# Softmax denominators of the first attention layer: from eight rows and a spreading product to all rows, inverted on GpSimd

## What is computed

```python
q = (layernorm(x) @ Wq)                 # 16 heads x 56 rows = 896 columns per batch
k, v = ctx @ Wk, ctx @ Wv               # 8 key/value heads
scores = einsum('bhtd,bhsd->bhts', q, k) / sqrt(128)
attn = softmax(scores, axis=-1)         # over 1500 context rows
out = einsum('bhts,bhsd->bhtd', attn, v) @ Wo
```

## Time and profile before

| what | us |
|---|---|
| median of 3 runs | 2184.47 (2183.3 to 2184.73) |
| the profiled execution, its own time | 2184.68 |
| its span, first to last instruction | 2182.9 |
| TensorE busy | 2129.5 (98%) |
| VectorE busy | 1566.5 (72%) |
| GpSimd busy | 1350.9 (62%) |
| ScalarE busy | 951.6 (44%) |

### The profile page before, as it was taken

One profiled execution on the slowest core, in us unless ns is written; L12 is line 12 of the kernel. 1 busy time (PEld: TensorE's weight loads), 2 busy tenths in 40 slices (PEclk: granted clock), 3 DMA queues, 4 the chain that ended last, 5 costly groups with the idle time before them and its releaser, 6 DMA issues. The chain is left out here.

```text
span 2182.9 us, 27103 instructions
## 1 busy us (share of the span) xinstructions
PE 2129.5 (98%) x8898; PEld 1565.0 (72%) x8898; DVE 1566.5 (72%) x2574; ACT 951.6 (44%) x2536; POOL 1350.9 (62%) x1056
## 2 busy tenths in 40 slices
PE   7999999999999999999999999899999999999999
PEld 6777777777777777777777655566666666665998
DVE  4689888988898888988896433656666666652577
ACT  3454454444444455444445225444444343431432
POOL 0378777877687767877787300088778787771221
PEclk9999999999999999999999999999999999999999
DMA  3000000000000000000001410011110111101110
GB/s 131 15 29 15 29 29 15 15 29 29 15 15 29 29 15 25 19 29 15 29 11 39 145 40 0 21 50 49 37 57 29 57 44 42 43 1 51 37 52 25
DMA packets 15134, 75.62 MB, mean 35 GB/s; under 512 B 1746, under 2 KB 2114, under 8 KB 13986
## 3 DMA queue, kind: packets, MB, share of 16 engines
q1 hardware_dynamic: 14994, 73.89, 10.4%
HBM read 72.97 MB, written 0.92 MB: 34 GB/s over the span
## 5 line engine op out<-in xcount | busy, mean ns | idle before, releaser
L618 POOL TENSOR_TENSOR l_prod<-l_prod 125x256 f32<-125x256 f32 x576 | 417.2, 738 | 270.6 <-DVE l_prod L683 270.0
L683 DVE TENSOR_TENSOR l_prod<-l_side,xq 125x512 f32<-125x512 f32 x576 | 394.5, 685 | 55.7 <-PE l_side L814 48.8
L959 POOL TENSOR_TENSOR l_acc<-l_acc,l_probs 125x896 f32<-125x896 f32 x160 | 346.0, 2163 | 81.4 <-ACT l_probs L909 65.6
L559 ACT ACTIVATE l_probs<-l_slots,mask_bias 125x448 f32<-125x448 f32 x384 | 238.1, 632 | 343.0 <-PE l_slots L753 342.9
L979 DVE TENSOR_TENSOR l_scaled<-l_slots,rk 125x896 f32<-125x896 f32 x192 | 207.0, 1084 | 197.8 <-PE l_slots L1044 197.6
L612 POOL TENSOR_TENSOR l_acc<-l_acc,l_probs 125x896 f32<-125x896 f32 x160 | 338.5, 2116 | 0.0
L541 ACT ACTIVATE l_prod_act<-l_prod_act 125x128 f32<-125x128 f32 x768 | 228.0, 298 | 235.5 <-DVE l_prod_act L683 235.4
L909 ACT ACTIVATE l_probs<-l_scaled 125x896 f32<-125x896 f32 x192 | 182.8, 952 | 320.7 <-DVE l_scaled L979 295.7
L692 DVE TENSOR_REDUCE l_msq<-l_prod 125x4 f32<-125x256 f32 x576 | 234.6, 410 | 1.6
L646 DVE SCALAR_TENSOR_TENSOR top<-l_side,mask_bias,top 125x448 f32<-125x448 f32 x330 | 223.1, 676 | 6.7 <-PE l_side L797 5.8
L1042 PE MATMUL l_slots<-l_qhi,l_clo 128*125 128x448 f32 x384 | 203.0, 529 | 1.4 <-DVE l_qlo L984 1.4
(11 more groups left out here) (241 smaller groups left out, 4374.6 us busy)
## 6 DMA issues: line engine op xcount, KB each, us to landing
land<-in_ctxT SPq DMA_DIRECT2D x32, 750.0 KB, 4.4
l_nat<-in_ctxN SPq DMA_DIRECT2D x16, 750.0 KB
post_we<-in_experts SPq DMA_DIRECT2D x20, 384.0 KB, 3.0
spare<-in_ctxN SPq DMA_DIRECT2D x8, 750.0 KB
nat<-in_ctxN SPq DMA_DIRECT2D x8, 750.0 KB
spare<-in_wo SPq DMA_DIRECT2D x2, 2048.0 KB, 7.8
spare<-in_wqT SPq DMA_DIRECT2D x4, 512.0 KB, 4.3
mid_fac<-in_factors SPq DMA_DIRECT2D x1, 2048.0 KB, 8.0
```

Of the source, the lines that this page charges most:

```text
L559: act.activation(P[t % NP][:, HALF * i:HALF * i + HALF], bank_of("S", t, i)[0:KT, 0:HALF], ACT.Exp, bias=m.mask_bias[:, b, t:t + 1]).then_ ...
L618: pool.tensor_tensor(buf[:, :, 0:C // 2], buf[:, :, 0:C // 2], buf[:, :, C // 2:C], ALU.add).then_inc(s.half_sum, 1)
L683: dve.tensor_tensor(to[:, :, :], bank, xt.unsqueeze(1).to_broadcast([KT, 4, C]), ALU.mult).then_inc(s.side_dve, 1)
L959: pool.tensor_tensor(acc[:, :], acc[:, :], P[t % NP][:, :], ALU.add).then_inc(s.acc, 1)
```

## The change

Bank "D" becomes two banks, one for each half. `sums` is now two products with an all-ones matrix (128 output rows, 448 columns each), so that the denominators stand on all rows at once, both at t = 0. `spread`, `m.inv` and VectorE's `invert` and `normalise` are gone. ScalarE copies both banks to a new SBUF buffer `den` at the start of step 1 (`sums_out`), ahead of the exponentials of tile 2. GpSimd then, in four pieces of 224 columns, one in each of the steps 6 to 9 between its `add` and its halvings, raises `den` to the power -1 and multiplies `qs` by it. For the last batch the four pieces follow behind the loop. In `ORDER` the entries "D", "E", "E" become "D", "D" and an unused one. `NPROD` goes from 5 to 4.

```diff
-NPROD, NPROD_ACT, LAG_N, NLOW = 5, 2, 3, 4
+NPROD, NPROD_ACT, LAG_N, NLOW = 4, 2, 3, 4
-ORDER = [("S", 0, 0), ("S", 0, 1), ("S", 1, 0), ("S", 1, 1), ("D", 0, 0), ("E", 0, 0), ("E", 0, 1)]
+ORDER = [("S", 0, 0), ("S", 0, 1), ("S", 1, 0), ("S", 1, 1), ("D", 0, 0), ("D", 0, 1), ("-", 0, 0)]
...
-                if kind == "D" and b > 0:
-                    return pe.wait_ge(s.inv, b)
-                if kind == "E" and b > 0:
-                    return pe.wait_ge(s.o_done, 2 * b - 1 + half)
+                if kind == "D" and b > 0:
+                    return pe.wait_ge(s.den_out, 2 * b - 1 + half)
...
+            def sums_out(b):
+                for half in range(2):
+                    act.wait_ge(s.den, 2 * b + half + 1)
+                    need(act, s.o_done, 4 * b)
+                    act.activation(den[:, half, :], bank_of("D", 0, half)[:, 0:HALF], ACT.Copy).then_inc(s.den_out, 1)
...
                 for t in range(NT):
+                    if t == 1 and b > 0:
+                        sums_out(b - 1)
...
+            sums_out(B - 1)
...
+            def normalise(b, i):
+                pool.wait_ge(s.o_raw, b + 1)
+                pool.wait_ge(s.den_out, 2 * b + i // 2 + 1)
+                cols = slice(HALF // 2 * i, HALF // 2 * (i + 1))
+                o = m.qs[:, b, :, :].rearrange("p h q -> p (h q)")[:, cols]
+                part = den[:, :, :].rearrange("p a c -> p (a c)")[:, cols]
+                pool.tensor_tensor(part, part, neg[:, :].to_broadcast([C, HALF // 2]), ALU.pow).then_inc(s.inv, 1)
+                pool.wait_ge(s.inv, 4 * b + i + 1)
+                pool.tensor_tensor(o, o, part, ALU.mult).then_inc(s.o_done, 1)
...
                     if t > 0:
                         add(b, t)
+                    if b > 0 and 6 <= t < 10:
+                        normalise(b - 1, t - 6)
...
+            for i in range(4):
+                normalise(B - 1, i)
...
-            def invert(b):
-                dve.wait_ge(s.den, b + 1)
-                dve.reciprocal(m.inv[0:QBLK, :], bank_of("D", 0, 0)[0:QBLK, 0:TT]).then_inc(s.inv, 1)
-            def normalise(b):
-                dve.wait_ge(s.o_raw, b + 1)
-                o = m.qs[:, b, :, :].rearrange("p (a h) q -> p a (h q)", a=2)
-                for half in range(2):
-                    dve.wait_ge(s.spread, 2 * b + half + 1)
-                    dve.tensor_tensor(o[:, half, :], bank_of("E", 0, half)[:, 0:HALF], o[:, half, :],
-                                      ALU.mult).then_inc(s.o_done, 1)
...
             def sums(b):
                 pe.wait_ge(s.acc, (NT - 1) * (b + 1))
-                wait_bank(pe, b + 1, "D", 0, 0)
-                for j in range(QBLK):
-                    last = pe.matmul(out[:, 0:TT], m.row_of[0:KT, 127 - j:255 - j], acc[:, TT * j:TT * j + TT],
-                                     start=j == 0, stop=j == QBLK - 1)
-            def spread(b):
-                ...
+                for half in range(2):
+                    wait_bank(pe, b + 1, "D", 0, half)
+                    pe.matmul(bank_of("D", 0, half)[:, 0:HALF], m.ones[0:KT, :], acc[:, HALF * half:HALF * half + HALF],
+                              start=True, stop=True).then_inc(s.den, 1)
```

More of the change, by code:

```diff
@@ L286, in side_job @@
                     if t == 0:
-                        dve.wait_ge(s.const, 5)
+                        dve.wait_ge(s.const, 4)
                         dve.tensor_scalar(m.top[:, cols], bank[0:KT, 0:HALF], bias, None, ALU.add).then_inc(s.side_dve, 1)
@@ L312, in _ @@
             dve.memset(m.ones_r[:, :].bitcast(F32), 1.0).then_inc(s.const, 1)
-            dve.memset(m.inv[:, :], 0.0).then_inc(s.const, 1)
             dve.memset(m.eps[:, :], RMS_EPS).then_inc(s.const, 1)
@@ L439, in first_attention @@
         "ld_land", "ld_nat0", "ld_nat1", "ctx_hi", "ctx_lo", "q_hi", "q_lo", "nat_hi", "xq", "shift",
-        "scores", "probs", "pv", "acc", "den", "inv", "spread", "o_raw", "o_done",
+        "scores", "probs", "pv", "acc", "den", "den_out", "neg", "inv", "o_raw", "o_done",
         "ld_wv", "ld_wo", "side_pe", "side_dve", "side_act", "half_sum", "sum_dve", "sum_act", "rk_pre"])
@@ L459, in first_attention @@
         msq = sb("msq", [KT, NT, H], F32)
+        den = sb("den", [C, 2, HALF], F32)
+        neg = sb("neg", [C, 1], F32)
         side = [psum(f"side{i}", [128, 512]) for i in range(3)]
@@ L606, in add @@
                 if t == 1:
-                    need(pool, s.den, b)
+                    need(pool, s.den, 2 * b)
                     pool.tensor_tensor(acc[:, :], P[0][:, :], P[1][:, :], ALU.add).then_inc(s.acc, 1)
@@ L618, in halve @@
                 pool.tensor_tensor(buf[:, :, 0:C // 2], buf[:, :, 0:C // 2], buf[:, :, C // 2:C], ALU.add).then_inc(s.half_sum, 1)
+            def normalise(b, i):
[7 more added lines that the diff above has]
+                pool.tensor_tensor(o, o, part, ALU.mult).then_inc(s.o_done, 1)
+            pool.memset(neg[:, :], -1.0).then_inc(s.neg, 1)
+            pool.wait_ge(s.neg, 1)
             for b in range(B):
@@ L726, in _ @@
                             jobs = jobs[1:]
-                        invert(b - 1)
                         twice_less_high(b)
-                    if t == 1 and b > 0:
-                        normalise(b - 1)
                     for n in jobs:
@@ L735, in _ @@
                             add_up(b, i)
-            invert(B - 1)
-            normalise(B - 1)
         @block.tensor
@@ L768, in sums @@
                 pe.wait_ge(s.acc, (NT - 1) * (b + 1))
-                wait_bank(pe, b + 1, "D", 0, 0)
-                out = bank_of("D", 0, 0)
-                for j in range(QBLK):
-                    last = pe.matmul(out[:, 0:TT], m.row_of[0:KT, 127 - j:255 - j], acc[:, TT * j:TT * j + TT],
-                                     start=j == 0, stop=j == QBLK - 1)
-                last.then_inc(s.den, 1)
-            def spread(b):
-                pe.wait_ge(s.inv, b + 1)
-                for half in range(2):
[L780 to L785, removed]
+                for half in range(2):
+                    wait_bank(pe, b + 1, "D", 0, half)
+                    pe.matmul(bank_of("D", 0, half)[:, 0:HALF], m.ones[0:KT, :], acc[:, HALF * half:HALF * half + HALF],
+                              start=True, stop=True).then_inc(s.den, 1)
             def side_job(n):
@@ L826, in side_jobs @@
                         del jobs[:count]
-                    if t == 1 and b > 0:
-                        spread(b - 1)
                     for half in range(2):
@@ L840, in _ @@
             sums(B - 1)
-            spread(B - 1)
 def second_attention(nc, m, a, tag, sem):
@@ L1761, in build @@
         m.row_of = sb("row_of", [128, 255], F32)
-        m.inv = sb("inv", [128, TT], F32)
         m.eps = sb("eps", [128, 1], F32)
```

## The result

The changed kernel takes 4408.29 us (median of 4 runs, 4405.93 to 4408.87), the kernel before 2184.28: a ratio of 2.018, 95% interval 2.0152 to 2.0209. The prediction was 2289, with a range from 2150 to 2500: the direction was right and the size wrong by far.

The account below looks back on a forecast made before the run. The prediction took TensorE as the bound, busy for 69.9 of a batch's 71.0 us. Its terms, -15 + 108 + 11 = +104 us on 2184.7, gave 2289 us, with a range from 2150 to 2500.

Parts of the forecast that it names:

- TensorE's columns: TensorE's `sums` and `spread`, 3.57 us together, become two products of 1.51 us: 2.06 us saved a batch by work alone.
- the wait for bank "D": At the batch boundary TensorE's second `sums` product waits for ScalarE's exponential of tile 1; new `sums` ends 1.6 us later.
- the gain: TensorE's saving at the 15 batch boundaries after the bank wait: 14 x 0.9 + 2.4 = 15 us.
- The last boundary: The last of 15 batch boundaries: no high parts made, ScalarE some 2 us earlier, so the full 2.4 us gained.
- ScalarE at nothing: ScalarE's two copies, some 0.6 us each, fit in its 5.29 us wait ahead of tile 2's exponential: cost nothing.
- The power's price: GpSimd's power on 224 columns: 3.1 us, from VectorE's reciprocal at 4.7 times its plain product.
- What a piece delays: In steps 6 to 9 pieces hold up GpSimd's halvings, then VectorE's sums and TensorE's side jobs: 108 us over 15 batches.
- the threshold: Piece time a batch beyond which the rest falls on TensorE whole: 6.5 us free plus 1.4 from side banks, 7.9.
- 4x: GpSimd's time for a batch's four pieces, each power, product and the wait between them, 3.8 us: 15.1 us.
- the prediction's own terms: Boundary gain -15, stall 15 x (15.1 - 7.9) = 108, and 11 us for the last batch's uncovered pieces (17.3 against 6.0).
- NPROD: With four product buffers VectorE waits for its own sums in steps 6 to 9: taken as nothing, at most 9 us.
- The Trainium skill's rule: Two-input elementwise work belongs on VectorE, GpSimd being about 2x slower; by this the power also costs 3.1 us.

Follow-up runs that it names:

- plain_op: The changed kernel with GpSimd's power replaced by a plain product with the same -1 operand: 2176.02 us, 0.9965 of the kernel before.
- log_exp: The changed kernel with ScalarE making the inverses by logarithm and exponential, the power gone from GpSimd: 2176.60 us, 0.9965 of the kernel before.
- power_8: The changed kernel with the power on only the first 8 of each piece's 224 columns: 2210.73 us, 1.012 of the kernel before.
- power_18: The changed kernel with the power on only the first 18 of each piece's 224 columns: 2309.97 us, 1.0574 of the kernel before.
- vector_inverse: The changed kernel with the second `sums` product at step 1's start and inverses by VectorE's reciprocal in steps 2 to 5: 2230.77 us, 1.0213.

## Why the prediction was right and wrong

1. **TensorE's columns and the wait for bank "D": right in kind, the gain somewhat too large.** The wait was found in the order list: 1.7 us for 1.9. The last boundary has one too, of 0.85 us, where the prediction had none. Over 15 batches `plain_op` gains 10.6 us for 15, and comes to 2176 for 2171.
2. **ScalarE at nothing: right.** With the copies done it still waits 3.19 us at that place in `plain_op`, and in `log_exp` table loads and exponentials, some 3.6 us more a batch at that place, cost 0.6 us in all.
3. **The power's price: wrong, and it is the step that failed.** The prediction took 3.1 us for 224 columns, carried over from VectorE's reciprocal by the ratio of plain operations, and ended its range at 6.3, a price that no run shows. The power measured 36.2, twelve times the one and six times the other. VectorE's reciprocal said nothing of GpSimd's power, and no row before bounded it from above. That the kernel would be slower came out right, since a power of 1.65 us already does that (`power_8`).
4. **What a piece delays: right in mechanism.** The queue behind it, and the stall at VectorE's sum and TensorE's side jobs, are as described; `power_18`, at about the price that the prediction took, measured 2310. That this lies within 6 us of the 2304 expected is in part luck: the fourth piece is 0.8 us longer in 14 batches (+12), and the threshold is 8.4 for 7.9 (-7.5).
5. **The sum with the measured price.** The pieces take 36.73 us each from start to start of the next work (1529.70 - 1492.97), and in 14 of the 15 batches the fourth 0.85 more: 4x = 147.8, and 146.9 in the last batch and behind it. By the prediction's own terms that is -15 + 14 x (147.8 - 7.9) + (146.9 - 7.9) + (2.2 + 146.9 - 6.0) = +2226, and 2184.7 + 2226 = 4410, for 4408 measured. Here too the gain and the threshold are off in opposite directions. From `plain_op`, with 8.4 as threshold, it is 2176 + 14 x 139.4 + 138.5 + (146.9 - 5.0) = 4408.
6. **NPROD: nearly right**, 2.4 us where nothing was taken and 9 allowed.
7. The Trainium skill's rule cited in the prediction ("GPSIMD Engine Reference", section 4.1), about 2x slower, gave the same 3.1 us. It holds for the plain rows and not for the power. Its direction, away from GpSimd, was right; VectorE, which it names, loses 2.1% as well (`vector_inverse`).

## What to carry to other kernels

An operation that no row shows has no upper price. When it would sit on an engine whose queue feeds the bound one, work out the price from which it decides (here 1.4 us for 224 columns), and time it alone before building around it. A stall is set by the work in front of the nearest deadline and not by an engine's idle share: GpSimd was idle for 24% of a batch, and 8 columns of the power (10.3 us a batch) already cost 1.2%. Where banks are used in turn, read for each new user the entry that stands one turn back; that gave the wait for bank "D", and moving one product to where that entry is done gave 8 to 10 us.

## What the runs showed of the hardware that was not expected

GpSimd's `pow` on fp32 costs 0.4 us and 159 ns a column (1.65, 3.23, 18.2 and 36.0 us for 8, 18, 112 and 224 columns), which is 74 times a plain operation's 2.15, and the same for 8 partitions as for 128.

The piece in step 9 is 0.85 us longer than the other three, whatever its size (36.88 for 36.03; the longest of 8 columns 2.51 for 1.65), in 14 of the 15 batches that have pieces. It is the one during which VectorE makes `shift` for the next batch, reading two SBUF operands. GpSimd's third and fourth piece of a batch, VectorE's `shift` in it, and the piece in step 9 of the last batch, which has no next one and so makes no `shift`, in the changed kernel:

```profile
1534.48 36.03 POOL L636 TENSOR_TENSOR l_den<-l_den,l_neg 128x224 f32<-128x224 f32 x1
1575.29 36.87 POOL L636 TENSOR_TENSOR l_den<-l_den,l_neg 128x224 f32<-128x224 f32 x1
...
1575.11 1.17 DVE L684 TENSOR_TENSOR shift<-negmax,ident 112x896 fp32r<-112x896 f32 x1
...
3251.19 36.03 POOL L636 TENSOR_TENSOR l_den<-l_den,l_neg 128x224 f32<-128x224 f32 x1
```

This `shift` starts 0.18 us ahead of GpSimd's fourth piece and takes 1.17 us where its median before was 1.09; in the first batch, which has no pieces, it takes 1.09 here too. Without a `shift` beside it the piece in step 9 takes 36.03, and with 8, 18 and 112 columns too it has its usual length in the last batch (1.65, 3.22 and 18.21). In `plain_op` the product in the power's place is over before `shift` starts (424.60 and 426.47 us in one batch) and keeps its 0.56 us. There `shift` falls beside a halving, and this is now the long one, 1.65 us for 0.74, so that three halvings take 3.11 us where three take 2.11 in the rows of `power_18`:

```profile
425.87 3.11 POOL L627 TENSOR_TENSOR l_prod<-l_prod 125x256 f32<-125x256 f32 x3
...
L627 POOL TENSOR_TENSOR l_prod<-l_prod x576: 720/739/1649, 89.4 to 1205.2; 125x256 f32<-125x256 f32 x192
```

So it is `shift` that delays GpSimd's instruction, and not the step: in the 0.99 us of overlap the power loses 0.85, and `shift` 0.08. Through what, these rows don't show. The Trainium skill, "GPSIMD Engine Reference", section 1, says that GpSimd's SBUF interfaces are shared with VectorE, with contention when a VectorE instruction has two SBUF inputs; these rows fit it.
